# A two-layer decoder on one core: the experts' down products two slots later, one table of expert results, a token choice with fused sums, and norms that add their squares in halves

## The chip, the cores and the metric

The kernel runs as one program on one core of a Trainium2 chip. The metric is the device time of one launch in microseconds (us). In these texts PE is TensorE, DVE is VectorE, ACT is ScalarE, POOL is GpSimd and SP is SyncE, which issues most of the DMAs.

## The reference

Two post-norm decoder layers over 2048 tokens (8 sequences of 256) of width 512. Layer 0 is an attention whose keys and values are kept only for the most important tokens, a WKV recurrence, and a mixture of experts with 4-bit weights. Layer 1 is a causal attention, a cross attention and a dense feed-forward. A layer norm follows each part. What the change touches computes this:

```python
# sparse attention, layer 0: which tokens keep their key and value
importance = (x @ Wi + bi)[..., 0]
threshold = sorted_desc[:, tidx][:, None]          # tidx = int(256 * 0.2)
sparse_mask = (importance > threshold)
_, top_idx = jax.lax.top_k(importance, 32)         # and the 32 highest in any case
sparse_mask = jnp.maximum(sparse_mask, min_mask)

# layer norm, six times
m = jnp.mean(x, axis=-1); v = jnp.var(x, axis=-1)
y = (x - m) / jnp.sqrt(v + 1e-5)

# mixture: 16 experts, 4 per token, and a shared expert for all tokens
# each expert: silu(gate) * up, 512 -> 384, then down 384 -> 512, weights in fp4
```

## The kernel before

Activations lie transposed in SBUF: `g.xt` ("residual") holds features on the 128 partitions, in C = 4 blocks, and the 2048 tokens along the free axis. The program is a list of stages, each a Block with a barrier of all engines at its end. Within a stage the order of each engine is written out by hand, and counting semaphores tie the engines together.

**The token choice** (`sparse_select`). DVE has the importance of all tokens on every partition (`imp`), with the partition as the token asked about. It takes its own token's importance (`own`, 16 columns: 8 sequences times 2 halves) and fills whole tables `ge` (others at least as important) and `gt` (others more important), each 4096 numbers a partition, then reduces, subtracts, masks with `tri` (others that come earlier) and reduces again. The count of those ahead decides whether a token is kept and in which slot. PE waits for the result `sel`.

**The norms** (`layer_norm`, numbered 0 to 5 by `layer`). Four tiles of 512 tokens each. Per tile: PE averages over features by a product with a constant matrix (`mean`, 4 matmuls), DVE subtracts (`centre`), ACT squares, PE averages the squares (`var`, 4 matmuls), ACT takes Ln and then Exp for the inverse root, DVE multiplies (`scale`). The norms 2 and 3 have a `prepare_next`: POOL works on the next stage's weights beside them. Norm 4 has a `fill_vector`: DVE decodes weights of the feed-forward between its own steps.

**The routing** (`route`). It writes the tokens, as two fp16 parts that sum to the value times 64, to `rows_dram`, and the value times 64 in f32 (`scaled`) as `kept` to the second of two tables `sum_dram[0]` and `sum_dram[1]`. `g.rows` names, for each slot of a routed tile, the token's row. An empty slot names a row behind the 2048 tokens, the same for both halves of a tile.

**The experts** (`experts`). 55 tiles of 256 slots: 8 of the shared expert over all tokens, then 47 routed ones. The work of a tile j is cut into 6 steps o, and all engines walk the same slots s = 6 j + o. In a slot PE does `group` (8 matmuls for 128 hidden features, gate or up), then one `down` (3 matmuls of a tile before: one half of the slots, one third of the hidden features), and in slots 1 and 3 a `turn` (8 transposes of the next tile's rows). `item = NO * (j - 1) + o - 2` says which down. What leads to a down is a chain over engines: ACT and DVE scale and add the group's results (L1348, L1406), POOL adds the halves (L1261), ACT takes silu (L1354), DVE multiplies (L1414), ACT rounds (`high`, L1361), DVE takes the rest (`low`, L1419), which is what `h_ready` counts. `out` moves a finished tile from PSUM to `y`. For a shared tile SP stores it to `sum_dram[0]`; for a routed one POOL scatters its halves by indirect DMAs that add, half k into table k (L1252). POOL's `gather` (L1240) loads the rows of tile j + 3. SP loads the weights of tile j + 2 when tile j - 1 has finished its downs (ring of three).

**The combining** (`combine`). SP loads both tables, DVE adds them, PE turns the sums back and ACT divides by 64 into `g.xt`.

```python
for n in range(G_I * j, G_I * (j + 1)):                  # POOL, tile j
    if j < N:
        pool.wait_ge(ev_dve, 4 * (n + 1)); ...           # the add of L1261
    if n % G_I == 0 and N_SHARED <= j + 3 < N: gather(j + 3)
    if n % G_I == 1 and N_SHARED <= j - 2: scatter(j - 2)
```

## Time and profile before

| | |
|---|---|
| median of 3 runs | 2708.68 us (2708.18 to 2710.73) |
| profiled execution | 2711.14 us, its span 2709.3 us |
| busy share: PE, DVE, ACT, POOL | 75%, 67%, 49%, 35% |
| mean granted clock of PE | 0.893 of full speed |

A row of a timeline gives the start in us from the span's start, the busy time in us, the engine, the line and operation, what it writes from what it reads, how many like it are merged, and in brackets the idle time of the engine just before it and what ended it. Rows of "x8" are eight instructions in a row. A row of the windows gives the stretch and its length, then busy us with the number of instructions for PE, PE's weight loads, DVE, ACT and POOL, then the granted clock of PE, the mean busy share of the 16 DMA engines, and GB/s. A row of a DMA queue gives its packets, MB and the share of 16 engines' time that its packets took; q0 carries POOL's indirect DMAs, q1 those of SP.

### The profile page before, as it was taken

How to read it: one execution, taken by the hardware profiler on the slowest of the kernel's cores; microseconds unless marked ns; L12 is line 12 of the kernel's file. 1: busy time of each engine (PE TensorE's matmuls, PEld its weight loads, DVE VectorE, ACT ScalarE, POOL GpSimd, SP SyncE). 2: the span in 40 equal slices, each digit the busy share in tenths (PEclk: the TensorE clock that was granted, in tenths of full speed). 3: DMA queues.
4: the chain of work that ended last, by engine and by line, in shares of the span. 5: the costliest groups of instructions: out<-in, count | busy, mean ns of one | idle time of the engine just before them, and what ended most of it. 6: DMA issues, size and time to landing. Idle time of an engine off the chain costs nothing. (4 is left out here: it accounts for less than half of the span.)

```text
span 2709.3 us, 33393 instructions
## 1 busy us (share of the span) xinstructions
PE 2043.6 (75%) x12168; PEld 1270.0 (47%) x12203; DVE 1814.1 (67%) x2409; ACT 1326.7 (49%) x2139; POOL 953.4 (35%) x547
## 2 busy tenths in 40 slices
PE   2788765126498898988956899997994776789986
PEld 1456642012366666666633566663552332344442
DVE  4349883875776777777744356654443897999975
ACT  0013232655376776766734223323553885556656
POOL 1014443213245777777735122224111000443330
PEclk7888887668699999999987999998997998899998
DMA  3224655001637999999964000002334530000001
GB/s 141 62 93 159 241 189 221 0 0 44 235 102 246 254 251 262 247 261 256 251 152 169 0 1 1 1 1 109 92 80 140 187 118 1 0 1 1 1 0 62
DMA packets 123684, 313.63 MB, mean 116 GB/s; under 512 B 29569, under 2 KB 49537, under 8 KB 119810
## 3 DMA queue, kind: packets, MB, share of 16 engines
q1 hardware_dynamic: 102466, 260.69, 27.8%
q0 software_dynamic: 21056, 50.84, 9.5%
q8 instruction: 96, 1.57, 0.2%
q14 instruction: 66, 0.54, 0.1%
HBM read 219.59 MB, written 92.68 MB: 115 GB/s over the span
## 5 line engine op out<-in xcount | busy, mean ns | idle before, releaser
L1406 DVE SCALAR_TENSOR_TENSOR x_part<-x_group,x_scale,x_part 128x256 f32<-128x256 f32 x660 | 287.9, 477 | 144.2 <-ACT x_part L1348 137.5
L1295 PE MATMUL x_group<-x_xt,x_gu 128*128 128x256 f16 x2640 | 346.2, 275 | 2.1 <-ACT x_part L1348 1.2
L1348 ACT ACTIVATE x_part<-x_group,x_scale 128x256 f32<-128x256 f32 x660 | 276.1, 471 | 123.5 <-PE x_group L1295 117.5
L1261 POOL TENSOR_TENSOR x_part<-x_part 128x512 f32<-128x512 f32 x165 | 235.4, 1431 | 196.7 <-DVE x_part L1406 196.7
L1295 PEld LDWEIGHTS x_group<-x_xt,x_gu 128*128 128x128 fp8e4 x2640 | 237.0, 98 | 85.9 <-issue 32.4
L1312 PE MATMUL x_y_ps<-x_d_hi,x_h_hi 128*128 128x512 f32 x330 | 160.0, 485 | 68.8 <-DVE x_h_lo L1419 66.8
L2418 POOL TENSOR_TENSOR f_part<-f_part 128x1024 f32<-128x1024 f32 x44 | 120.4, 2737 | 188.0 <-DVE f_part L2445 188.0
L154 PE MATMUL mean_n<-residual,const_tables 128*128 128x512 f32 x160 | 79.3, 648 | 138.6 <-PEq L733 103.5
L1754 POOL TENSOR_TENSOR c_pt<-c_pt,const_tables 128x1024 f32<-128x1024 f32 x32 | 75.8, 2369 | 258.4 <-ACT c_pt L1728 258.4
L2316 PE MATMUL f_group<-f_x_hi,f_raw 128*128 128x512 f16 x352 | 138.9, 394 | 32.1 <-DVE f_part L2445 24.6
L1252 POOL DMA_INDIRECT mixed_rows<-x_y,moe_rows x94 | 150.1, 1597 | 31.0 <-issue 20.8
L2182 ACT ACTIVATE z_pt<-z_s 128x1024 f32<-128x1024 f32 x128 | 119.7, 1052 | 51.5 <-PE z_s L2153 50.4
L2445 DVE SCALAR_TENSOR_TENSOR f_part<-f_group,f_scale,f_part 128x512 f32<-128x512 f32 x176 | 123.9, 742 | 26.8 <-ACT f_part L2367 21.1
L2316 PE MATMUL f_group<-f_x_lo,f_raw 128*128 128x512 f16 x352 | 138.0, 392 | 0.0
L2367 ACT ACTIVATE f_part<-f_group,f_scale 128x512 f32<-128x512 f32 x176 | 111.0, 679 | 44.2 <-PE f_group L2316 44.0
L1312 PE MATMUL x_y_ps<-x_d_lo,x_h_hi 128*128 128x512 f32 x330 | 131.1, 397 | 0.0
L1312 PE MATMUL x_y_ps<-x_d_hi,x_h_lo 128*128 128x512 f32 x330 | 130.2, 395 | 0.0
L154 PEld LDWEIGHTS mean_n<-residual,const_tables 128*128 128x128 f32 x160 | 32.9, 209 | 181.6 <-issue 181.6
L1240 POOL DMA_INDIRECT x_row<-token_rows,moe_rows x94 | 102.5, 1091 | 21.5 <-issue 16.4
L1312 PEld LDWEIGHTS x_y_ps<-x_d_hi,x_h_hi 128*128 128x128 f32 x330 | 62.5, 189 | 98.0 <-DVE x_h_lo L1419 92.8
L199 ACT ACTIVATE squares_n<-centred_n 128x2048 f32<-128x2048 f32 x24 | 45.9, 1911 | 127.5 <-DVE centred_n L177 127.5
L2330 PE MATMUL f_y<-f_h_hi,f_w_hi 128*128 128x512 f32 x176 | 104.9, 596 | 3.2 <-DVE f_h_lo L2457 2.2
(331 smaller groups left out, 5042.3 us busy)
## 6 DMA issues: line engine op xcount, KB each, us to landing
x_d_hi<-down_hi SPq DMA_DIRECT2D x50, 768.0 KB, 5.7
x_d_lo<-down_lo SPq DMA_DIRECT2D x50, 768.0 KB, 5.9
x_gu<-codes_gu SPq DMA_DIRECT2D x50, 384.0 KB, 5.7
p_w<-d_s SPq DMA_DIRECT2D x17, 768.0 KB, 7.7
down_hi<-p_hi SPq DMA_DIRECT2D x17, 768.0 KB, 3.9
down_lo<-p_lo SPq DMA_DIRECT2D x17, 768.0 KB, 6.3
aux<-ct SPq DMA_DIRECT2D x2, 4096.0 KB, 16.3
cross_values<-y_v_out SPq DMA_DIRECT2D x16, 512.0 KB, 3.0
```

Source lines behind the costliest of these rows:

```text
L154: mm = pe.matmul(mean_ps[t % 2][:, :], g.const("mean"), tile(src, t)[:, c, :], start=c == 0, stop=c == C - 1)
L1252: pool.indirect_dma_start(out=g.sum_dram[k], out_offset=bass.IndirectOffsetOnAxis(ap=g.rows[:, at:at + 1], axis=0), in_=y[u][:, k, :], in_ ...
L1261: pool.tensor_tensor(x[:, 0, :, :], x[:, 0, :, :], x[:, 1, :, :], ALU.add).then_inc(summed, 1)
L1295: mm = pe.matmul(group_ps[s % 2][:, q, :], codes[:, q, col:col + P], xt[u][:, k, q, :], start=k == 0, stop=k == 1)
L1312: mm = pe.matmul(y_ps[half][:, :], x[u][:, k, rows], w[v][:, k, :], start=k == 0 and i == 0, stop=k == G_I - 1 and i == 2)
L1348: act.activation(part[n % PARTS][:, q, o % 2, :], group_ps[s % 2][:, q, :], ACT.Copy, scale=scale[v][:, o, q:q + 1]).then_inc(ev_act, 1)
L1406: dve.scalar_tensor_tensor(x, group_ps[s % 2][:, 2 + q, :], scale[v][:, o, 2 + q:3 + q], x, ALU.mult, ALU.add).then_inc(ev_dve, 1)
L2182: act.activation(pt[n % RING_P][:, :, :, :], s_ps[n % 3][:, :, :, :], ACT.Exp, scale=HDX ** -0.5)\
L2316: mm = pe.matmul(group_ps[c][:, :], codes[:, n, C * k + c, :], x[t % 2][:, c, :], start=i == 0, stop=i == 1)
L2367: act.activation(part[N % PARTS][:, c, k, :], group_ps[c][:, :], ACT.Copy, scale=scale[:, N % G_F, k, c:c + 1]).then_inc(ev_act, 1)
L2418: pool.tensor_tensor(x[:, 0, :, :], x[:, 0, :, :], x[:, 1, :, :], ALU.add).then_inc(summed, 1)
L2445: dve.scalar_tensor_tensor(x, group_ps[c][:, :], scale[:, N % G_F, k, c:c + 1], x, ALU.mult, ALU.add)\
```

## The change

It has four parts.

In `experts`, `DOWN_LAG = 4` takes the place of the 2 in the number of the down that a slot does. ACT's `out` moves from slot 0 to slot 2, DVE's from slot 2 to slot 4, and POOL's `scatter` from behind the second add of a tile to behind the third.

The two tables of results become one, with 128 spare rows for each half of a tile, so that the two halves' empty slots name different rows. The copy `kept` is dropped: `combine` loads the one table in 8 pieces, PE turns it, and DVE divides by 64 and adds to the residual in one instruction from PSUM. ACT has no part in it.

In the choice, each of the 16 columns has three SCALAR_TENSOR_TENSOR of 256 elements that compare, mask and sum in one instruction (`accum_out`), and the tables `ge` and `gt` are only written, in fp16. `later` (1 minus `tri`) is made ahead of it, while DVE waits for `imp`.

In the norms, DVE's `pair` adds the squares of blocks 0, 1 to those of 2, 3, in place, for the norms without `prepare_next` (0, 1, 4 and 5), and `var` is 2 matmuls there. PE does three tiles' `mean` before the first `var`, and DVE's order is written out anew. All six norms get an Ln of one column (`primed`) ahead of the wait for `var`.

```diff
@@ layer_norm
+        halved = prepare_next is None
+        base_pairs, ahead = g.pairs, 2 if halved else 1
...
             def var(t):
-                pe.wait_ge(squares_ready, base + t + 1)
+                if halved:
+                    pe.wait_ge(paired, base_pairs + t + 1)
+                else:
+                    pe.wait_ge(squares_ready, base + t + 1)
...
-                for c in range(C):
+                terms = C // 2 if halved else C
+                for c in range(terms):
...
-            mean(0)
+            for t in range(ahead):
+                mean(t)
             for t in range(NT):
-                if t + 1 < NT:
-                    mean(t + 1)
+                if t + ahead < NT:
+                    mean(t + ahead)
                 var(t)
...
+            def pair(t):
+                if halved:
+                    dve.wait_ge(squares_ready, base + t + 1)
+                    x = squares[t % 2]
+                    dve.tensor_tensor(x[:, 0:2, :], x[:, 0:2, :], x[:, 2:4, :], ALU.add).then_inc(paired, 1)
...
             for t in range(NT):
+                act.activation(primed[:, :], eps, ACT.Ln)
                 act.wait_ge(var_ready, base + t + 1)
@@ sparse_select
-                dve.tensor_tensor(ge[:, :, q, :], imp[:, :, :], mine, ALU.is_ge)
-                last = dve.tensor_tensor(gt[:, :, q, :], imp[:, :, :], mine, ALU.is_gt)
...
-            step(dve.tensor_reduce(n_gt, gt[:, :, :, :].rearrange("p b q j -> p (b q) j"), AX.X, ALU.add))
...
+            for n in range(2 * B):
+                b, q, mine = n // 2, n % 2, own[:, n:n + 1]
+                earlier = g.const("tri")[:, q * S:(q + 1) * S]
+                dve.scalar_tensor_tensor(ge[:, n, :], imp[:, b, :], mine, ones, ALU.is_ge, ALU.mult,
+                                         accum_out=n_ge[:, n:n + 1])
+                dve.scalar_tensor_tensor(gt[:, 0, n, :], imp[:, b, :], mine, earlier, ALU.is_ge, ALU.mult,
+                                         accum_out=ties[:, n:n + 1])
+                last = dve.scalar_tensor_tensor(gt[:, 1, n, :], imp[:, b, :], mine, later[:, q * S:(q + 1) * S],
+                                                ALU.is_gt, ALU.mult, accum_out=after[:, n:n + 1])
             step(last)
-            step(dve.tensor_tensor(ties, ties, n_gt, ALU.add))
+            step(dve.tensor_tensor(ties, ties, after, ALU.add))
@@ route
-                sp.dma_start(kept[:, n:n + 4, :], scaled[:, n:n + 4, :]).then_inc(stored, 16)
@@ experts
-                    pool.indirect_dma_start(out=g.sum_dram[k], out_offset=bass.IndirectOffsetOnAxis(ap=g.rows[:, at:at + 1], axis=0),
+                    pool.indirect_dma_start(out=g.sum_dram, out_offset=bass.IndirectOffsetOnAxis(ap=g.rows[:, at:at + 1], axis=0),
...
-                    if n % G_I == 1 and N_SHARED <= j - 2:
+                    if n % G_I == 2 and N_SHARED <= j - 2:
                         scatter(j - 2)
...
-                item = NO * (j - 1) + o - 2
+                item = NO * (j - 1) + o - DOWN_LAG
...
-                if o == 0 and 2 <= j < N + 2:
+                if o == DOWN_LAG - 2 and 2 <= j < N + 2:
                     out(j - 2)
...
-                if o == 2 and 2 <= j < N + 2:
+                if o == DOWN_LAG and 2 <= j < N + 2:
                     out(j - 2)
@@ combine
-    NTOK, GROUP = T // P, 4
+    NTOK, GROUP = T // P, 2
...
+                dve.scalar_tensor_tensor(x, turn_ps[n % 4][:, :, :], 1.0 / X_GAIN, x, ALU.mult, ALU.add).then_inc(out, 1)
```

PE in the expert stage, where tile 5 (its weights in `gu2`) is in its slots 2 and 3; `d_hi1` are the down weights of tile 4 and `d_hi0` those of tile 3. Before:

```order
L1312 MATMUL x_y_ps0<-x_d_hi1,x_h_hi0 128x512 [waits x_y0_out,x_h_ready,x_d_landed1]
L1312 MATMUL x_y_ps0<-x_d_hi1,x_h_lo0 128x512
L1312 MATMUL x_y_ps0<-x_d_lo1,x_h_hi0 128x512
L1295 MATMUL x_group1<-x_xt1,x_gu2 128x256 [waits x_ev_act]
L1295 MATMUL x_group1<-x_xt1,x_gu2 128x256 x3
L1295 MATMUL x_group1<-x_xt1,x_gu2 128x256 [waits x_ev_dve]
L1295 MATMUL x_group1<-x_xt1,x_gu2 128x256 x3
L1312 MATMUL x_y_ps0<-x_d_hi1,x_h_hi0 128x512 [waits x_h_ready]
```

and at the same place of the changed kernel:

```order
L1347 MATMUL x_y_ps1<-x_d_hi0,x_h_hi1 128x512
L1347 MATMUL x_y_ps1<-x_d_hi0,x_h_lo1 128x512
L1347 MATMUL x_y_ps1<-x_d_lo0,x_h_hi1 128x512
L1330 MATMUL x_group1<-x_xt1,x_gu2 128x256 [waits x_ev_act]
L1330 MATMUL x_group1<-x_xt1,x_gu2 128x256 x3
L1330 MATMUL x_group1<-x_xt1,x_gu2 128x256 [waits x_ev_dve]
L1330 MATMUL x_group1<-x_xt1,x_gu2 128x256 x3
L1347 MATMUL x_y_ps1<-x_d_hi0,x_h_hi1 128x512
```

The downs beside the same groups are those of two slots earlier: they end tile 3 where they began tile 4, and no wait for `h_ready` stands in these two slots.

POOL at the end of the expert stage, where the last tiles are scattered. Before:

```order
L1261 TENSOR_TENSOR x_part3<-x_part3 128x512 [waits x_ev_dve]
L1252 DMA mixed_rows0<-x_y0,moe_rows 2176x512 [waits x_y0_out,x_y_mixed1]
L1252 DMA mixed_rows1<-x_y0,moe_rows 2176x512 [waits x_y1_out]
L1261 TENSOR_TENSOR x_part0<-x_part0 128x512 [waits x_ev_dve]
L1252 DMA mixed_rows0<-x_y1,moe_rows 2176x512 [waits x_y0_out,x_y_mixed0]
L1252 DMA mixed_rows1<-x_y1,moe_rows 2176x512 [waits x_y1_out]
L1252 DMA mixed_rows0<-x_y0,moe_rows 2176x512 [waits x_y0_out,x_y_mixed1]
L1252 DMA mixed_rows1<-x_y0,moe_rows 2176x512 [waits x_y1_out]
```

and changed:

```order
L1296 TENSOR_TENSOR x_part3<-x_part3 128x512 [waits x_ev_dve]
L1296 TENSOR_TENSOR x_part0<-x_part0 128x512 [waits x_ev_dve]
L1287 DMA mixed_rows<-x_y0,moe_rows 2304x512 [waits x_y0_out,x_y_mixed1]
L1287 DMA mixed_rows<-x_y0,moe_rows 2304x512 [waits x_y1_out]
L1287 DMA mixed_rows<-x_y1,moe_rows 2304x512 [waits x_y0_out,x_y_mixed0]
L1287 DMA mixed_rows<-x_y1,moe_rows 2304x512 [waits x_y1_out]
L1287 DMA mixed_rows<-x_y0,moe_rows 2304x512 [waits x_y0_out,x_y_mixed1]
L1287 DMA mixed_rows<-x_y0,moe_rows 2304x512 [waits x_y1_out]
```

The scatter that stood between the second and third add of the last tile stands behind the third; all name one table.

DVE in norm 0. Before:

```order
L177 TENSOR_TENSOR centred0_n0<-residual,mean0_n0 128x2048 [waits ln_mean_ready]
L177 TENSOR_TENSOR centred1_n0<-residual,mean1_n0 128x2048 [waits ln_mean_ready]
L177 TENSOR_TENSOR centred2_n0<-residual,mean0_n0 128x2048 [waits ln_mean_ready]
L190 TENSOR_TENSOR residual<-centred0_n0,rs0_n0 128x4x512 [waits ln_rs_ready]
L177 TENSOR_TENSOR centred3_n0<-residual,mean1_n0 128x2048 [waits ln_mean_ready]
L190 TENSOR_TENSOR residual<-centred1_n0,rs1_n0 128x4x512 [waits ln_rs_ready]
L190 TENSOR_TENSOR residual<-centred2_n0,rs0_n0 128x4x512 [waits ln_rs_ready]
L190 TENSOR_TENSOR residual<-centred3_n0,rs1_n0 128x4x512 [waits ln_rs_ready]
```

and changed, where rows that write `squares` are the additions in halves:

```order
L186 TENSOR_TENSOR centred0_n0<-residual,mean0_n0 128x2048 [waits ln_mean_ready]
L186 TENSOR_TENSOR centred1_n0<-residual,mean1_n0 128x2048 [waits ln_mean_ready]
L193 TENSOR_TENSOR squares0_n0<-squares0_n0 128x1024 [waits ln_squares_ready]
L186 TENSOR_TENSOR centred2_n0<-residual,mean0_n0 128x2048 [waits ln_mean_ready]
L193 TENSOR_TENSOR squares1_n0<-squares1_n0 128x1024 [waits ln_squares_ready]
L186 TENSOR_TENSOR centred3_n0<-residual,mean1_n0 128x2048 [waits ln_mean_ready]
L193 TENSOR_TENSOR squares0_n0<-squares0_n0 128x1024 [waits ln_squares_ready]
L197 TENSOR_TENSOR residual<-centred0_n0,rs0_n0 128x4x512 [waits ln_rs_ready]
L193 TENSOR_TENSOR squares1_n0<-squares1_n0 128x1024 [waits ln_squares_ready]
L197 TENSOR_TENSOR residual<-centred1_n0,rs1_n0 128x4x512 [waits ln_rs_ready]
L197 TENSOR_TENSOR residual<-centred2_n0,rs0_n0 128x4x512 [waits ln_rs_ready]
L197 TENSOR_TENSOR residual<-centred3_n0,rs1_n0 128x4x512 [waits ln_rs_ready]
```

The first tile is scaled behind the fourth tile's subtraction, not ahead of it, and the second only when all four additions are done.

## Rows read from the trace of the kernel before

**Rows 1.** Windows: busy time by stretch, first a shared stretch, then one routed tile.

```profile
780.00:800.00 20.00, 17.93 (x141) 13.39 (x138) 13.82 (x34) 14.08 (x34) 10.41 (x9) 1.00 0.34 103
1200.00:1212.08 12.08, 10.87 (x82) 8.03 (x82) 9.25 (x23) 8.47 (x20) 9.31 (x7) 1.00 0.92 258
```

**Rows 2.** Timeline of PE in the expert stage: start us, us, engine line op.

```profile
738.07 0.50 PE L1312 MATMUL x_y_ps<-x_d_hi,x_h_hi 128*128 128x512 f32 x1 [1.76 <-DVE x_h_lo L1419]
...
833.29 0.50 PE L1312 MATMUL x_y_ps<-x_d_hi,x_h_hi 128*128 128x512 f32 x1 [1.48 <-DVE x_h_lo L1419]
...
1206.75 1.05 PE L1295 MATMUL x_group<-x_xt,x_gu 128*128 128x256 f16 x8
...
1208.33 0.62 PE L1279 MATMUL x_turn<-x_ident,x_row 128*128 128x128 f16 x8
1208.79 1.04 PE L1295 MATMUL x_group<-x_xt,x_gu 128*128 128x256 f16 x8
...
1212.62 0.50 PE L1312 MATMUL x_y_ps<-x_d_hi,x_h_hi 128*128 128x512 f32 x1 [1.21 <-DVE x_h_lo L1419]
...
1380.57 0.50 PE L1312 MATMUL x_y_ps<-x_d_hi,x_h_hi 128*128 128x512 f32 x1 [0.66 <-DVE x_h_lo L1419]
```

**Rows 3.** Timeline of POOL over one routed tile.

```profile
1209.43 1.28 POOL L1261 TENSOR_TENSOR x_part<-x_part 128x512 f32<-128x512 f32 x1 [1.49 <-DVE x_part L1406]
...
1213.77 1.27 POOL L1261 TENSOR_TENSOR x_part<-x_part 128x512 f32<-128x512 f32 x1 [0.36 <-DVE x_part L1406]
```

**Rows 4.** DMA queues over four routed tiles, 1200 to 1248.32 us.

```profile
q1 hardware_dynamic: 2892, 8.02, 48.1%
q0 software_dynamic: 1792, 4.33, 44.0%
```

**Rows 5.** Timeline of the expert stage's end, POOL and DVE.

```profile
1383.15 1.56 POOL L1252 DMA_INDIRECT mixed_rows<-x_y,moe_rows  x1
...
1384.19 0.88 DVE L1406 SCALAR_TENSOR_TENSOR x_part<-x_group,x_scale,x_part 128x256 f32<-128x256 f32 x2
...
1390.28 1.56 POOL L1252 DMA_INDIRECT mixed_rows<-x_y,moe_rows  x1 [2.41 <-DMA mixed_rows<-x_y,moe_rows]
```

**Rows 6.** Timeline of DVE in the token choice.

```profile
41.98 2.29 DVE L322 TENSOR_TENSOR s_ge<-s_imp,s_own 128x2048 f32<-128x2048 f32 x1
...
73.28 0.17 DVE L335 TENSOR_SCALAR s_small<-s_small 128x16 f32<-128x16 f32 x1
```

**Rows 7.** Timeline of DVE: two nearby kinds of instruction, 256 elements each.

```profile
687.56 0.69 DVE L1034 TENSOR_TENSOR_SCAN r_running<-const_tables,r_total 128x256 f32<-128x256 f32 x1
...
1200.74 0.87 DVE L1406 SCALAR_TENSOR_TENSOR x_part<-x_group,x_scale,x_part 128x256 f32<-128x256 f32 x2
```

**Rows 8.** Timeline of the combining stage, issue to last eviction.

```profile
1410.22 0.38 SPq L1485 DMA_DIRECT2D m_mixed<-mixed_rows  x1
...
1418.44 2.50 DVE L1492 TENSOR_TENSOR m_mixed<-m_mixed,m_kept 128x512 f32<-128x512 f32 x4 [24.42 <-DMA m_kept<-mixed_rows]
...
1424.75 3.64 PE L1501 MATMUL m_turn<-const_tables,m_mixed 128*128 128x128 f32 x16 [1.89 <-DVE m_mixed L1492]
...
1438.41 1.14 ACT L1508 ACTIVATE residual<-m_turn 128x512 f32<-128x512 f32 x2 [0.26 <-PE m_turn L1501]
```

**Rows 9.** Timeline of ACT and DVE in the first norm, and after it.

```profile
473.67 1.92 ACT L199 ACTIVATE squares_n<-centred_n 128x2048 f32<-128x2048 f32 x1 [2.17 <-DVE centred_n L177]
...
480.54 1.91 ACT L199 ACTIVATE squares_n<-centred_n 128x2048 f32<-128x2048 f32 x1 [1.01 <-DVE centred_n L177]
...
490.36 2.29 DVE L190 TENSOR_TENSOR residual<-centred_n,rs_n 128x2048 f32<-128x2048 f32 x1 [1.65 <-ACT rs_n L210]
...
493.19 0.20 ACT L784 ACTIVATE w_fade<-w_fade 128x4 f32<-128x4 f32 x1
```

**Rows 10.** Timeline of the third norm's end: DVE and POOL.

```profile
1470.10 7.24 DVE L190 TENSOR_TENSOR residual<-centred_n,rs_n 128x2048 f32<-128x2048 f32 x2 [1.48 <-ACT rs_n L210]
...
1482.07 4.49 POOL L1552 TENSOR_TENSOR c_wk<-c_wk,c_wkr 128x2048 f32<-128x2048 f32 x1
```

More of the change, by code:

```diff
@@ L178, in centre, with scale @@
                                   ALU.subtract).then_inc(centred_ready, 1)
-            if fill_vector is not None:
-                fill_vector(dve, 0)
-            centre(0)
-            centre(1)
-            for t in range(NT):
-                if t + 2 < NT:
-                    centre(t + 2)
-                if fill_vector is not None and t >= 1:
-                    fill_vector(dve, t)
+            def pair(t):
[3 more added lines that the diff above has]
+                    dve.tensor_tensor(x[:, 0:2, :], x[:, 0:2, :], x[:, 2:4, :], ALU.add).then_inc(paired, 1)
+            def scale(t):
                 dve.wait_ge(rs_ready, base + t + 1)
@@ L191, in _, with fill @@
                                   ALU.mult).then_inc(normed, 1)
+            def fill(t):
+                if fill_vector is not None:
+                    fill_vector(dve, t)
+            fill(0)
+            centre(0)
+            centre(1)
+            pair(0)
+            centre(2)
+            pair(1)
+            fill(1)
+            if halved:
+                centre(3)
+                pair(2)
+                scale(0)
+                pair(3)
+            else:
+                scale(0)
+                centre(3)
+            fill(2)
+            scale(1)
+            fill(3)
+            scale(2)
+            scale(3)
         @block.scalar
@@ L313, in _ @@
             dve.tensor_copy(wib[:, :, :], bc(wi[:, :], 2, [P, C, P])).then_inc(wib_ready, 1)
+            dve.tensor_scalar(later[:, :], g.const("tri"), -1.0, 1.0, ALU.mult, ALU.add)
             dve.wait_ge(imp_copied, NT)
@@ L922, in _ @@
             out = g.rows_dram[0:T, :].rearrange("(n p) f -> p n f", p=P)
[L923 to L926 removed]
+            for k in range(HALVES):
+                spare = slice(T + k * P, T + (k + 1) * P)
+                sp.dma_start(g.rows_dram[spare, :], a["one_row"][:, 0:ROW].to_broadcast([P, ROW])).then_inc(stored, 16)
+                sp.dma_start(g.sum_dram[spare, :], a["one_row"][:, 0:D].to_broadcast([P, D])).then_inc(stored, 16)
             for n in range(0, NTOK, 4):
@@ L1066, in _ @@
             dve.wait_ge(rows_found, 1)
-            step(dve.tensor_scalar(empty[:, :], row_ps, 0.0, g.const("spare"), ALU.is_equal, ALU.mult))
+            for k in range(HALVES):
+                last = dve.tensor_scalar(empty[:, k::HALVES], row_ps[:, k::HALVES], 0.0, g.const("spare")[:, k:k + 1],
+                                         ALU.is_equal, ALU.mult)
+            step(last)
             dve.scalar_tensor_tensor(g.rows[:, :], empty[:, :], -1.0, row_ps, ALU.add, ALU.add)
@@ L1480, in _ @@
         def _(sp):
+            rows = g.sum_dram[0:T, :].rearrange("(n p) f -> p n f", p=P)
             for i, s in enumerate(landed):
                 part = slice(i * GROUP, (i + 1) * GROUP)
-                for dst, src in ((mixed, g.sum_dram[0]), (kept, g.sum_dram[1])):
-                    rows = src[0:T, :].rearrange("(n p) f -> p n f", p=P)
-                    sp.dma_start(dst[:, part, :], rows[:, part, :]).then_inc(s, 16)
-        @block.vector
-        def _(dve):
-            for n in range(NTOK):
-                if n % GROUP == 0:
-                    dve.wait_ge(landed[n // GROUP], 32)
-                dve.tensor_tensor(mixed[:, n, :], mixed[:, n, :], kept[:, n, :], ALU.add).then_inc(summed, 1)
+                sp.dma_start(mixed[:, part, :], rows[:, part, :]).then_inc(s, 16)
         @block.tensor
@@ L1496, in _ @@
             for n in range(NTOK):
[L1497 removed]
+                if n % GROUP == 0:
+                    pe.wait_ge(landed[n // GROUP], 16)
                 if n >= 4:
```

57 lines of the change are left out of this document (23 added, 34 removed).

## The prediction

> **What bounds the kernel now.** I began with the page (busy shares, the slices, the groups), then took the waits of the expert stage, the timelines of the places that the diff touches, the windows for a price per tile, and the DMA queues. No engine is busy throughout: the page's 75% for PE is an average over stages that end on different things, so each edit is priced at its own place.
>
> The experts take a quarter of the time, 55 tiles in a row. In a routed tile of 12.08 us PE is busy 10.87, and DVE, ACT and POOL 9.3, 8.5 and 9.3; the DMA engines are at 0.92, against 0.34 in a shared stretch [rows 1]. What ends PE's idle time, once a tile, is DVE's `low`: the second down of a tile waits 1.21 us for it, behind a group [rows 2]. Without this wait a slot is a group and a down, 1206.75 to 1208.33, 1.58 us, and a turn 0.46 (to 1208.79): six slots and two turns make 10.4 us [rows 2]. So each tile loses about 1.7 us to a chain that passes ACT and DVE several times and POOL once, while every one of them has time left. The granted clock there is 1.00, the 2.4 GHz level [rows 1], so nothing is to be had from the clock.
>
> The other three places are serial. The choice is one chain on DVE from 41.98 to 73.28 us, with PE waiting [rows 6]. The combining starts its loads at 1410.22 and sees the first 2 MB land at 1418.44 [rows 8]. The norms are a chain over PE, DVE and ACT.
>
> **The experts, in four steps.** The three items of `down` that wait for `h_ready` come two slots later, and so do the two `out`s and the scatter: no distance between them changes, only that from `low` to its down, from one slot to three. Two slots are over 3.1 us, the wait 1.21, so it goes. What is late next? PE may run two slots ahead of the evictions of `group_ps`. By hand, with DVE's 9.25 us in a tile of 10.4, DVE has 1.1 us left [rows 1], and its heaviest slot (group, out, low, product) is followed by slots with less. ACT has more. So the floor of PE, 10.4 us, is reachable as far as compute goes.
> - Shared tiles: from the stall at 738.07 to that at 833.29 are 8 periods of 11.90 us [rows 2]. DMA is at 0.34, no limit. I take 10.55 a period: 8 x 1.35 = 10.8 us off.
> - Routed tiles: 833.29 to 1380.57 hold 45 periods, 12.16 on average [rows 2], 12.08 in steady state [rows 1]. Two limits stand close under that. POOL waits 1.49 and 0.36 us in a tile [rows 3], so its adds, gathers and scatters with their issue take 12.08 - 1.85 = 10.2 us. And the DMA engines: over four tiles (48.3 us) the packets took 48.1% and 44.0% [rows 4], that is 11.1 us a tile. The shares of the two queues sum to that of the windows, so packets of one do not lie beside packets of the other on an engine, and if their durations stay, 11.1 us is the least that a tile can take in the long run. It is not felt at once: weights are asked for some 13 slots before use, over 20 us, and a backlog of 11.1 - 10.5 a tile needs more than 20 tiles to use that up. I take 10.6 to 10.7 for the first half and 11.2 for the second, 10.95 on average: 45 x (12.08 - 10.95) = 50.9 us off.
> - The last group comes two downs earlier, 2 x 0.78 = 1.6 us off.
> - The end: the scatter that stood behind the second add of the last tile stands behind the third. Before, it was issued at 1383.15, and the next only at 1390.28, when its DMA had landed: three pairs, each some 7 us behind the other, end the stage [rows 5]. The last groups' eviction starts at 1384.19 and takes 0.88; with the add of 1.27 [rows 3] the chain of scatters starts near 1386.4, 3.3 us later. 3.3 us on.
>
> Sum of the experts: 10.8 + 50.9 + 1.6 - 3.3 = 60.0 us off. Bounds of the routed period: PE's 10.4 (75.6 us instead of 50.9) and 11.6, where the DMA share of 11.1 meets jitter (21.6).
>
> **The choice.** What goes is 31.3 us, 41.98 to 73.28 [rows 6]. What comes is 48 instructions of 256 elements and one addition of some 0.2. The trace has none that sums on the side. From below: a comparison of 2048 elements takes 2.29 us [rows 6], so 256 take at least 0.29, 13.7 us in all. From above: the scan, a DVE instruction that carries a value from element to element, takes 0.69 for 256 [rows 7], 33 us. The nearest in kind is the SCALAR_TENSOR_TENSOR of 256, two in 0.87 [rows 7], 0.44 with its own latency in it; behind each other they overlap, so I take 0.40: 19.2 + 0.2 = 19.4, and 11.9 us off (17.4 off to 2 on). The table `later` is made while DVE waits for `imp`, as it did before.
>
> Two statements of the Trainium skill speak against this part. "Vector Engine (DVE) Microarchitecture Reference", section "Points that are easy to get wrong", says that a SCALAR_TENSOR_TENSOR with two non-bf16 SBUF sources runs at half throughput, since no port is left for the accumulator's readback; and "VectorE: DVE Perf Modes", in its section on two Vector instructions with no wait between them, counts an operation that writes out its accumulator as two instructions. No run here shows either so far; by the first an instruction would take about twice its 0.29, an estimate of 0.58, and this part would give 3 us.
>
> **The combining.** Now 29.3 us (1410.22 to 1439.55) [rows 8]. Half the bytes, eight pieces of 512 KB instead of pairs of 1 MB. The first 2 MB land 8.2 us after the issue; a quarter of it lands after 8.2/4 = 2.1 at the least and I take 4.2. Then PE has 16 turns without a gap: four take 3.64 [rows 8], so 14.6, and the last eviction some 0.7: 19.5, 9.8 us off. PE is the bound of it, as the 4 MB land at twice the pace. The 16 additions of DVE that go, and ACT's copies, lay between; the new ones lie beside PE. The four stores of `kept` end long before the routing does, so dropping them gives nothing; one more small instruction on `empty` costs 0.1.
>
> **The norms.** In norm 0, ACT waits 2.17 and 1.01 us for DVE's subtraction, which waits for `mean`, which stood behind a `var` [rows 9]. With `mean` first and `var` half as long these 3.2 us go, and ACT, with three table loads and activations a tile, is the bound to the end. `primed` adds a small ACT instruction a tile; the nearest takes 0.20 [rows 9], 0.8 at most. So 3.2 - 0.8 leaves 2.4; I take 2.2 for the norms 0, 1 and 5, and 1.8 for norm 4, where DVE's decoding stands before its second scale: 8.4 off. The additions (DVE, four a norm, 1.2 each by half of a 2048-element product of 2.29 [rows 9]) lie beside ACT. Norm 2 ends with POOL, 1486.56 against DVE's 1477.34 [rows 10]: `primed` costs nothing. Norm 3 pays 0.6. Sum: 7.8 off.
>
> **The sum.** 60.0 + 11.9 + 9.8 + 7.8 = 89.5 us. Against the profiled execution's own 2711.1: 2621.6. The median of the runs is 2.4 below that one, so 2619.
>
> **The rivals.**
> 1. DMA is the bound of routed tiles throughout (11.2 to 11.6 a tile), through POOL: a scatter may not start before the last has landed, and POOL's adds wait behind it. For it: 0.92 at 12.08, and the second scatter already lands some 7 us after the first's issue [rows 1, 4, 5]. Against it: in a steady tile POOL waits for DVE alone [rows 3]. At 11.4: 30.6 instead of 50.9, 2639.
> 2. PE's floor is reached, the packets shorten or overlap: 10.45 a tile, 73 off, 2597. For it: q1's 8.02 MB in 48.1% of 48.3 us are 345 GB/s, q0's 4.33 in 44.0% only 204 [rows 4]; scatter packets may be mostly latency that a fuller queue hides.
> 3. The fused sums cost what the scan does, 0.69: 2 us on instead of 11.9 off, 2633.
> 4. The change doesn't do what it says: the wait for `low` comes back as a wait for evictions, because POOL's adds come behind two scatters in a row and silu and DVE follow. Period 11.8 or more: 12.6 instead of 50.9, 2657.
> 5. Slower. Scatters and weight loads meet in time, since weights are asked for two slots later as well; a pair of scatters then lands after more than a period, and POOL's wait sets the pace. The rest of the change gives 11.9 + 9.8 + 7.8 + 9.1 = 38.6, so it decides from 12.08 + 38.6/45 = 12.94 a tile on; with pairs of 13.3 us (now some 7) it would be 2725.
>
> **How the numbers follow.** Chances: the forecast (2606 to 2630) 0.42, DMA-bound 0.22, PE's floor 0.20, the scan's price 0.06, no gain in routed tiles 0.06, slower 0.03, and 0.01 for no change. The time is that of the forecast, 2619. The range takes in PE's floor and the dearer DMA case with the scan's price: 2592 to 2652. The forecast's own is 2606 to 2630. What a measurement of this kernel can tell from no change is about 0.2%, 5.4 us. Faster 0.96, same 0.01, slower 0.03.
>
> **What the changed profile would show.** In the routed stretch no wait of PE for `x_h_lo`, and a period near 10.9, with DMA over 0.97; if the period is 10.45, DMA under 0.97 refutes the fixed packet times; if it is 11.4, POOL's L1287 waits for its own DMA. Periods near 10.55 in shared tiles. 48 instructions in the choice, 19 us from first to last. The combining in 19.5 us with PE without gaps. 2.2 us less in norm 0, with no ACT wait for `centred`. The scatter chain at the end 3.3 us later behind the last group. Wrong it would be above all by the routed period: each 0.1 us is 4.5 us.

## The result, and the profile after

The changed kernel takes 2634.37 us (median of 3 runs, 2634.15 to 2637.72) against 2708.68; the ratio is 0.9728, 95% interval 0.9706 to 0.975. Forecast were 2619, in a range of 2592 to 2652; the measured time is 15 us above the forecast. The profiled execution took 2634.15 us with a span of 2632.2, that is 77.1 off the span where the sum had 89.5: 12.4 of the 15 us. Another 2.4 are what the forecast took off because the profiled execution of before stood that much above its median; after the change the two are level.

Where it came from, in us of the profiled spans. A term is read between two rows that both kernels have; copy k is DVE's one copy of `x_xt` for tile k. The forecast up to copy 13 is 8 shared periods and 4 routed ones (10.8 + 4.5), then 41 times 1.13.

| stretch | before | after | change | forecast |
|---|---|---|---|---|
| choice: first comparison to PE's `s_row` | 36.46 | 24.99 | -11.5 | -11.9 |
| norms 0, 1, 5: first subtraction to last scale | 30.47 | 27.43 | -3.04 each | -2.2 each |
| norm 4, the same | 30.47 | 27.91 | -2.6 | -1.8 |
| norm 3, the same | 30.47 | 30.65 | +0.2 | +0.6 |
| experts, copy 0 to copy 13 (shared, and the first routed) | 154.09 | 139.11 | -15.0 | -15.3 |
| experts, copy 13 to copy 54: 41 routed periods | 495.42 | 471.35 | -24.1 | -46.3 |
| last copy to the combining's first load | 39.26 | 43.91 | +4.7 | +1.7 |
| combining to norm 2's first `mean` | 29.64 | 16.19 | -13.5 | -9.8 |
| unchanged code elsewhere | | | -6.3 | 0 |

The row that fails is that of the routed tiles. Their period is 11.50 us, the same to 0.02 in nearly every tile, where it was 12.08 and the forecast had 10.95. The windows of after, a shared stretch and one routed tile (columns as in [rows 1]):

```profile
760.00:780.00 20.00, 20.00 (x160) 15.34 (x159) 15.27 (x38) 15.36 (x39) 10.57 (x10) 1.00 0.34 104
1157.27:1168.78 11.51, 10.87 (x86) 7.87 (x84) 10.02 (x23) 8.03 (x20) 9.06 (x7) 1.00 0.93 267
```

In the shared stretch PE has no gap left. In the routed tile the DMA share is 0.93 against 0.92, and POOL is busy for less than in [rows 1], but DVE has gone from 9.25 us to 10.02 in a shorter tile, with the same 23 instructions. PE's timeline of this tile has no wait for `x_h_lo` any more and two new ones. The first is put down to issue in PE's row, but the row of its weight load (PEld) names DVE's eviction:

```profile
1163.56 0.61 PE L1330 MATMUL x_group<-x_xt,x_gu 128*128 128x256 f16 x4 [0.33 <-issue]
1163.56 0.33 PEld L1330 LDWEIGHTS x_group<-x_xt,x_gu 128*128 128x128 fp8e4 x4 [0.61 <-DVE x_part L1441]
...
1167.32 0.61 PE L1330 MATMUL x_group<-x_xt,x_gu 128*128 128x256 f16 x4 [0.31 <-DVE x_part L1441]
```

DVE's timeline shows why the evictions are late, with POOL's beneath it:

```profile
1159.87 0.87 DVE L1441 SCALAR_TENSOR_TENSOR x_part<-x_group,x_scale,x_part 128x256 f32<-128x256 f32 x2 [1.35 <-ACT x_part L1383]
1160.66 1.72 DVE L1454 TENSOR_TENSOR x_h_lo<-x_h,x_h_hi 128x256 fp32r<-128x256 f32 x1
1162.30 0.41 DVE L1449 TENSOR_TENSOR x_h<-x_part 128x256 f32<-128x256 f32 x1
1162.64 0.86 DVE L1441 SCALAR_TENSOR_TENSOR x_part<-x_group,x_scale,x_part 128x256 f32<-128x256 f32 x2
...
1165.46 0.68 DVE L1454 TENSOR_TENSOR x_h_lo<-x_h,x_h_hi 128x256 fp32r<-128x256 f32 x1
...
1166.40 0.86 DVE L1441 SCALAR_TENSOR_TENSOR x_part<-x_group,x_scale,x_part 128x256 f32<-128x256 f32 x2
...
1168.48 0.42 DVE L1454 TENSOR_TENSOR x_h_lo<-x_h,x_h_hi 128x256 fp32r<-128x256 f32 x1
```

```profile
1157.27 1.63 POOL L1287 DMA_INDIRECT mixed_rows<-x_y,moe_rows  x1 [0.15 <-issue]
1159.21 1.58 POOL L1287 DMA_INDIRECT mixed_rows<-x_y,moe_rows  x1 [0.30 <-issue]
1160.25 1.84 POOL L1296 TENSOR_TENSOR x_part<-x_part 128x512 f32<-128x512 f32 x1
...
1164.57 1.28 POOL L1296 TENSOR_TENSOR x_part<-x_part 128x512 f32<-128x512 f32 x1
```

The same `low` takes 0.42, 0.68 and 1.72 us. The two long ones start while POOL's add runs and end 0.29 us after it does (the add ends at 1162.09 and `low` at 1162.38; 1165.85 and 1166.14). The evictions behind them end at 1163.50 and 1167.26, and PE's two waits end 0.06 us later. The kernel before had this once a tile, in DVE's and POOL's timelines; the add ends at 1207.93, `low` at 1208.23:

```profile
1207.26 0.97 DVE L1419 TENSOR_TENSOR x_h_lo<-x_h,x_h_hi 128x256 fp32r<-128x256 f32 x1
```

```profile
1206.08 1.85 POOL L1261 TENSOR_TENSOR x_part<-x_part 128x512 f32<-128x512 f32 x1
```

Over the stage `low` averaged 567 ns before (164 of them) and 840 ns after:

```profile
L1454 DVE TENSOR_TENSOR x_h_lo<-x_h,x_h_hi 128x256 fp32r<-128x256 f32 x164 | 137.7, 840 | 0.5 <-ACT x_h_hi L1396 0.5
```

From 1159.87 to 1170 DVE has hardly any idle time, and PE, two slots ahead of it, waits for its evictions.

The choice, in DVE's timeline (answers to [rows 6]); each sum has a row of its own:

```profile
40.67 0.48 DVE L359 SCALAR_TENSOR_TENSOR s_ge<-s_imp,s_own,const_tables 128x256 f16<-128x256 f32 x1
41.08 0.08 DVE L359 DVE_READ_ACCUMULATOR s_ge<-s_imp,s_own,const_tables 128x1 f32 x1
41.08 0.48 DVE L361 SCALAR_TENSOR_TENSOR s_gt<-s_imp,s_own,const_tables 128x256 f16<-128x256 f32 x1
...
60.29 0.18 DVE L366 TENSOR_TENSOR s_small<-s_small 128x16 f32<-128x16 f32 x1
```

48 instructions in 19.6 us, 0.41 from start to start. The combining (answers to [rows 8]):

```profile
1356.58 4.20 SPq L1516 DMA_DIRECT2D m_mixed<-mixed_rows  x8
1360.38 5.82 PE L1526 MATMUL m_turn<-const_tables,m_mixed 128*128 128x128 f32 x32 [25.23 <-DMA m_mixed<-mixed_rows]
...
1370.47 1.09 PE L1526 MATMUL m_turn<-const_tables,m_mixed 128*128 128x128 f32 x8 [0.20 <-DMA m_mixed<-mixed_rows]
...
1372.77 7.11 PE L158 MATMUL mean_n<-residual,const_tables 128*128 128x512 f32 x16 [1.21 <-PEq L1501]
```

Each of the last four pieces comes 1.3 to 1.4 us after the one before, and PE takes its two turns in 1.09 us and waits for the next. The first turns were slower: four of them took 3.8 us, 0.42 us a matmul against 0.27 later. The windows of PE's work on four turns before and of the first turns after show the same granted clock, 0.50 (the 1.2 GHz level); in the last turns it is 1.00 (2.4 GHz):

```profile
1424.75:1428.00 3.25, 3.25 (x15) 3.25 (x16) 1.75 (x3) 1.59 (x3) 0.00 (x0) 0.50 1.05 390
```

```profile
1360.38:1363.30 2.92, 2.86 (x12) 2.46 (x13) 1.39 (x2) 0.00 (x0) 0.00 (x0) 0.50 1.03 390
1369.17:1370.26 1.09, 1.08 (x8) 0.86 (x8) 1.08 (x3) 0.00 (x0) 0.00 (x0) 1.00 0.06 21
```

PE had been idle for 25.23 us ahead of the first turn, and for 1.89 us ahead of the four in [rows 8]. The norm, ACT and then DVE in norm 0 (answers to [rows 9]):

```profile
458.74 1.89 ACT L231 ACTIVATE squares_n<-centred_n 128x2048 f32<-128x2048 f32 x1
460.65 1.28 ACT L236 ACT_TABLE_LOAD   x1
461.95 0.20 ACT L236 ACTIVATE primed_n<-const_tables 128x1 f32<-128x1 f32 x1
462.06 0.67 ACT L241 ACTIVATE rs_n<-var_n,const_tables 128x512 f32<-128x512 f32 x1
```

```profile
447.14 2.29 DVE L186 TENSOR_TENSOR centred_n<-residual,mean_n 128x2048 f32<-128x2048 f32 x1 [24.30 <-PE mean_n L158]
...
474.56 2.29 DVE L197 TENSOR_TENSOR residual<-centred_n,rs_n 128x2048 f32<-128x2048 f32 x1 [1.74 <-ACT rs_n L243]
```

Behind its second squaring ACT has no wait any more in this norm; `primed` lies 0.11 us before the next start. The tail of the experts, POOL's timeline (answers to [rows 5]):

```profile
1328.87 1.56 POOL L1287 DMA_INDIRECT mixed_rows<-x_y,moe_rows  x1 [0.15 <-issue]
...
1336.18 1.55 POOL L1287 DMA_INDIRECT mixed_rows<-x_y,moe_rows  x1 [3.89 <-DMA mixed_rows<-x_y,moe_rows]
...
1343.48 1.55 POOL L1287 DMA_INDIRECT mixed_rows<-x_y,moe_rows  x1 [3.88 <-DMA mixed_rows<-x_y,moe_rows]
```

### The profile page after: what moved, and what is told of

Its sections match the earlier page's. It is cut to its first block and busy times, and to the rows that moved or that the text cites. A ratio compares the mean times of both kernels' runs of the same rounds, so it can differ in the third digit from the quotient of the medians.

```text
span 2632.2 us, 33369 instructions
## 1 busy us (share of the span) xinstructions
PE 2009.7 (76%) x12104; PEld 1245.7 (47%) x12139; DVE 1850.9 (70%) x2514; ACT 1297.3 (49%) x2147; POOL 945.4 (36%) x547
## 5 line engine op out<-in xcount | busy, mean ns | idle before, releaser
L1330 PE MATMUL x_group<-x_xt,x_gu 128*128 128x256 f16 x2640 | 362.0, 275 | 33.4 <-DVE x_part L1441 17.9
L1330 PEld LDWEIGHTS x_group<-x_xt,x_gu 128*128 128x128 fp8e4 x2640 | 229.4, 98 | 140.6 <-issue 60.0
L1383 ACT ACTIVATE x_part<-x_group,x_scale 128x256 f32<-128x256 f32 x660 | 264.5, 472 | 10.8 <-PE x_group L1330 10.6
L1396 ACT ACTIVATE x_h_hi<-x_h 128x256 fp32r<-128x256 f32 x165 | 68.8, 417 | 166.6 <-DVE x_h L1449 141.0
L1454 DVE TENSOR_TENSOR x_h_lo<-x_h,x_h_hi 128x256 fp32r<-128x256 f32 x165 | 138.2, 837 | 0.5 <-ACT x_h_hi L1396 0.5
## 6 DMA issues: line engine op xcount, KB each, us to landing
aux<-ct SPq DMA_DIRECT2D x2, 4096.0 KB, 15.3
```

The lines of the kernel that those rows point to most:

```text
L1330: mm = pe.matmul(group_ps[s % 2][:, q, :], codes[:, q, col:col + P], xt[u][:, k, q, :], start=k == 0, stop=k == 1)
L1383: act.activation(part[n % PARTS][:, q, o % 2, :], group_ps[s % 2][:, q, :], ACT.Copy, scale=scale[v][:, o, q:q + 1]).then_inc(ev_act, 1)
L1454: dve.tensor_tensor(h_lo[j % 2][:, n % G_I, :], h[n % 2][:, :], h_hi[j % 2][:, n % G_I, :].bitcast(F32), ALU.subtract).then_inc(h_ready, 1)
```

## The experiments

All times are medians, beside runs of the kernel before on the same chip (2709.9 to 2710.3). "Split" is the changed kernel with the edit of `split_scatter`.

| run | us | routed period, mean of 41 | DVE's `low`, mean ns from 700 to 1330 us |
|---|---|---|---|
| changed kernel | 2634.4 | 11.50 | 840 |
| lag2 | 2672.1 | 12.07 | 553 |
| lag3 | 2635.0 | 11.50 | 822 |
| low_one_input | 2620.8 | 11.17 | 406 |
| low_product_one | 2596.6 | 10.63 | 409 |
| split_scatter | 2595.9 | 10.52 | 445 |
| lag2_split | 2661.8 | 11.86 | 415 |
| split_early_weights | 2586.3 | 10.55 | 467 |
| split_light_weights | 2587.7 | 10.44 | 433 |
| best | 2586.4 | | |

**lag2: the lag undone.**

```diff
-    DOWN_LAG = 4
+    DOWN_LAG = 2
...
-                    if n % G_I == 2 and N_SHARED <= j - 2:
+                    if n % G_I == 1 and N_SHARED <= j - 2:
```

> The changed kernel with one part undone: the downs one slot behind again (DOWN_LAG 2), both outs two slots earlier and the scatter behind the second add of a tile. Theory (the later down gave 39 us between the first and the last tile and took 4 to 5 us back at the tail): routed tiles at 12.08 us again instead of 11.50, shared tiles at 11.8 instead of 10.4 to 10.6, so about 35 us longer than the changed kernel, 2669. Rival (part of the gain in the stage comes from the single table or its spare rows, not from the lag): routed tiles stay clearly under 12.0 and the time under 2660.

2672.1 us, 37.7 longer, routed 12.07 and shared 11.8. The stage's gain is the lag's; the one table and its spare rows have no part in it.

**lag3: one slot more, not two.** `DOWN_LAG = 3`, scatter as in lag2.

> The changed kernel with the down one slot later than before instead of two (DOWN_LAG 3), outs in slots 1 and 3, and the scatter behind the second add of a tile, as before the change. Theory: two slots, 3.1 us, still cover the 1.2 us that the down waited for low; the adds, gathers and scatters of POOL stand as before, where low was held up by 0.56 us a tile instead of 1.6, so DVE is busy 9.2 to 9.5 us and the routed period is 10.7 to 11.1, the tail 4 us shorter: about 2608. Rival (DMA-bound): 11.5, 2630. Rival (a lag of one slot more is not enough): PE waits for x_h_lo again, 11.5 to 12.

2635.0 us, 11.50 a tile and `low` at 822 ns. The tail is 4.5 us shorter, as expected, and given back ahead of copy 13 (2.2 us) and of the stage (2.5). So the scatter's new place is not what holds `low` longer: once PE stops waiting, DVE and POOL fall into the same pattern with the scatters behind the second add too. That part of the theory fell.

**low_one_input: `low` with one operand from SBUF.**

```diff
-                dve.tensor_tensor(h_lo[j % 2][:, n % G_I, :], h[n % 2][:, :], h_hi[j % 2][:, n % G_I, :].bitcast(F32),
-                                  ALU.subtract).then_inc(h_ready, 1)
+                    dve.tensor_reduce(h_lo[j % 2][:, n % G_I, :], h[n % 2][:, :].rearrange("p (m o) -> p m o", o=1),
+                                      AX.X, ALU.add).then_inc(h_ready, 1)
```

> The changed kernel, but DVE's low is a reduction over one element of h alone: same length, one SBUF input instead of two. It leaves the subtraction of h_hi out. Theory (low is held up until POOL's add beside it has ended, 1.3 and 0.3 us in a tile, DVE then runs behind and PE waits for its evictions): low takes about 0.41 us everywhere, DVE is busy 8.4 instead of 10.0 us in a tile, and the routed period falls from 11.50 to 10.4 to 10.9; with 10.6 some 40 us less, about 2594. Rival (the DMA engines, busy 0.93 of the time, set the 11.50): low is short, but the period stays at 11.5 and the time at 2634. Rival (POOL's own chain of adds, gathers and scatters sets it): the same 11.5, with POOL waiting for nothing.

2620.8 us, period 11.17. The time fell by 13.6 us, a third of the 40 that were expected. DVE's timeline, and the add of POOL beside it:

```profile
1152.38 0.41 DVE L1455 TENSOR_REDUCE x_h_lo<-x_h 128x256 fp32r<-128x256 f32 x1
1152.70 1.40 DVE L1449 TENSOR_TENSOR x_h<-x_part 128x256 f32<-128x256 f32 x1
```

```profile
1151.98 1.83 POOL L1296 TENSOR_TENSOR x_part<-x_part 128x512 f32<-128x512 f32 x1
```

`low` now runs beside the add at its full pace. The hold went to the product behind it, the next instruction with two operands from SBUF: 1.40 us, again to 0.29 after the add's end.

**low_product_one: the product as well.** Its `tensor_tensor` becomes the same kind of reduction.

> The changed kernel with both DVE instructions that read two operands from SBUF in the chain made into reductions over one element with one operand: low (leaves out the subtraction of h_hi) and product (leaves out the multiplication by up). Lengths stay 0.41 us when undisturbed. Theory (any DVE instruction with two SBUF inputs that meets POOL's add is held until the add ends; with low alone changed, the product took over 0.98 and 0.27 us of the hold, and the period only fell to 11.17): no hold is left, DVE is busy 8.4 to 8.6 us a tile, period 10.4 to 10.6, about 2593 us. Rival (POOL's pair of scatters makes the add late, and the late sum itself, through silu and product, sets the period whatever DVE does): low and product are both 0.41 but the period stays at 11.0 or more, 2612 or above.

2596.6 us, period 10.63 (29 of the 41 lie under 10.6, many at 10.3), both instructions at 0.41. DVE and POOL at the same place of a tile:

```profile
1076.74 0.41 DVE L1456 TENSOR_REDUCE x_h_lo<-x_h 128x256 fp32r<-128x256 f32 x1
1077.07 0.41 DVE L1449 TENSOR_REDUCE x_h<-x_part 128x256 f32<-128x256 f32 x1
```

```profile
1075.12 1.58 POOL L1287 DMA_INDIRECT mixed_rows<-x_y,moe_rows  x1 [0.30 <-issue]
1076.17 1.86 POOL L1296 TENSOR_TENSOR x_part<-x_part 128x512 f32<-128x512 f32 x1
```

POOL's order is that of the changed kernel, its add still stands behind two scatters and has the same 1.8 us, and still the tile is 0.87 us shorter. So neither POOL's chain nor the DMA engines made the 11.50: the hold on DVE did.

**split_scatter: the same by the order alone, with nothing left out.**

```diff
-                    if n % G_I == 2 and N_SHARED <= j - 2:
-                        scatter(j - 2)
+                    if n % G_I in (1, 2) and N_SHARED <= j - 2:
+                        scatter(j - 2, n % G_I - 1)
```

The second argument is the half.

> The changed kernel, but POOL scatters the first half of a tile behind the second add and the second half behind the third add, so that no add stands behind two scatters. Theory (POOL's add of the next tile comes late behind the pair of scatters, and so falls on DVE's low): the add is on time, low is held up less, routed period 10.7 to 11.1, about 2612 us. Rival (DMA-bound): 11.5 and 2634. Rival (the halves then wait for the landing of the tile before, as the last scatter is issued later against the next first one): POOL waits for its own DMA in every tile, period 12 or more, above 2650.

2595.9 us, 38.5 less than the changed kernel and more than was expected. Each add now stands behind one scatter or the gathers, POOL's timeline:

```profile
1152.13 1.28 POOL L1297 TENSOR_TENSOR x_part<-x_part 128x512 f32<-128x512 f32 x1 [0.56 <-DVE x_part L1442]
1153.57 1.57 POOL L1288 DMA_INDIRECT mixed_rows<-x_y,moe_rows  x1 [0.16 <-issue]
1154.91 1.54 POOL L1297 TENSOR_TENSOR x_part<-x_part 128x512 f32<-128x512 f32 x1
```

and the adds end as DVE comes to `low`, or before: the first `low` starts at 1153.27, 0.14 us ahead of the add's end, and takes 0.43 us, the second starts at 1156.96, 0.5 us behind it, and takes 0.41. What is left of PE's waits from 900 to 1250 us is that for `x_scale`, 3.8 us in 6 times.

**lag2_split: the split without the lag.** `DOWN_LAG = 2` in the split version.

> The version with split scatters, with the down back at its old place (DOWN_LAG 2, outs in slots 0 and 2); the halves of a tile are scattered behind the second and the third add. Theory (two separate limits: the wait of PE for low, which only the lag removes, and the hold of DVE beside POOL, which only the split removes): PE waits for x_h_lo again, about 1.2 us a tile, routed period 11.7 to 12.0, about 2660 to 2672 us. Rival (the scatters in a pair were what made low late before the change as well, so the split alone would have done): period 10.5 to 11, under 2625 us.

2661.8 us. `low` is short, and PE waits for it as before, once a tile, in its timeline:

```profile
1115.39 0.50 PE L1348 MATMUL x_y_ps<-x_d_hi,x_h_hi 128*128 128x512 f32 x1 [1.01 <-DVE x_h_lo L1455]
```

Without the lag the split gives 10.3 us, with it 38.5. The lag gives 37.7 alone and 65.9 with the split. Two limits stood one behind the other, and the change removed the first.

**split_early_weights and split_light_weights: what the DMA engines have to do with it.**

```diff
                 if N_SHARED <= j + 2 < N:
-                    e = expert(j + 2)
-                    gate_up(j + 2, e)
-                    down(j + 2, e)
+                    gate_up(j + 2, expert(j + 2))
+                if N_SHARED <= j + 1 < N:
+                    down(j + 1, expert(j + 1))
```

> The version with split scatters, and SP asks for the gate and up weights of tile j + 2 ahead of the down weights of tile j + 1, so they are not queued behind the wait for y_done, which the lag moved two slots back. In the split version PE waits for x_scale in some tiles (3.8 us from 900 to 1250 us) and periods of 10.42 alternate with 10.98. Theory (the scale is only late, as it is asked for 9 slots ahead): the waits go, period 10.42 throughout, 4 us less than 2596. Rival (the DMA engines, busy 0.99 of the time, are the limit and the wait only moves to another transfer): within 1 us of 2596.

The other loads one third of `d_lo` for routed tiles, the rest of the split version unchanged.

> The version with split scatters, with the low part of the down weights of routed tiles loaded for one third only (256 KB instead of 768 KB a tile, two thirds of the values are those of an earlier expert). Theory of the prediction (packet times are a load on the DMA engines that ends up as the limit near 11.1 us a tile): refuted already by 10.52; what is left of it is the wait for x_scale, which goes with a quarter of the weight bytes, period 10.42, about 2592 us, DMA share 0.8. Rival (no DMA limit at all, the waits come from the order of issue): the same 2596 with the same waits.

2586.3 and 2587.7 us. The windows from 900 to 1250 us, of early and then of light:

```profile
900.00:1250.00 350.00, 349.62 (x2719) 263.38 (x2717) 288.97 (x731) 269.76 (x662) 302.33 (x232) 1.00 1.00 293
```

```profile
900.00:1250.00 350.00, 350.00 (x2752) 266.58 (x2750) 285.86 (x736) 273.32 (x671) 303.99 (x235) 1.00 0.91 244
```

With a sixth of the bytes gone the period is 10.44 and nearly without jitter; with all of them it is 10.52 or 10.55, whatever the order of asking. So near 10.5 us the DMA engines do share the limit, for 0.1 us a tile: 3.3 of the light version's 8.2 us lie in the 41 periods, 3.8 ahead of them. The waits for `x_scale` went with the earlier asking, as expected, but waits of POOL for its own DMA grew instead (16.2 us in 20 times, 8.3 in 12 in the split version), so the steady part gained nothing. Of the early version's 9.6 us, 8.4 come from elsewhere: copy 8 to copy 13 takes 61.1 us in the split version, where POOL's first scatter waits 7.26 us for the last shared tile's store, issued by SP behind weights, and 52.7 in the early one, where it waits for no DMA.

**looks and mean_order: the small terms.** The first leaves `primed` out, adds eight SCALAR_TENSOR_TENSOR without a sum, and loads the combining in four pieces; the second has `ahead = 1` for all norms. Each ran once; `looks` took 2639.0 us, with eight instructions more in the choice.

> Three small edits of the changed kernel in stages that don't touch each other, each read from its own stage. (1) The six Ln of one column (primed) are gone. Theory: in a norm bound by ACT each costs its 0.11 us of pitch and hides nothing, since the table load stood ahead of the wait before the change too, so norm 0 is 0.4 us shorter; rival: it takes the table load off the path, and without it the norm is 1 us or more longer. (2) Eight SCALAR_TENSOR_TENSOR of 256 elements without a sum stand among the 48 with one. Theory: start to start both take 0.41 us, so the sum costs nothing; rival: the plain one takes 0.33 or less and the accumulator is paid for. (3) The combining loads four pieces of 1 MB instead of eight of 512 KB. Theory: the stage is bound by its 4 MB at some 400 GB/s, so it ends about one piece's worth of turns later, 1 to 2.5 us; rival: bound by PE's turns, the first piece lands 2 us later and all else follows by as much or more.

Norm 0 is 27.06 us instead of 27.42, and so are norms 1 and 5; norm 3 is 30.47 instead of 30.65. There `primed` costs 0.36 and 0.18 us and hides nothing. In norm 4 it is the other way: 28.14 us without it, 27.91 with it. Without it ACT starts its last load of the Ln table only when DVE, busy with its decoding, has scaled a tile. With `primed` that load lies ahead of the wait. ACT in norm 4 of `looks`:

```profile
2220.98 1.28 ACT L240 ACT_TABLE_LOAD   x1 [1.10 <-DVE residual L197]
```

The plain instruction and the one with a sum, in DVE's timeline:

```profile
41.30 0.49 DVE L360 SCALAR_TENSOR_TENSOR s_plain<-s_imp,s_own,const_tables 128x256 f16<-128x256 f32 x1
41.70 0.48 DVE L361 SCALAR_TENSOR_TENSOR s_ge<-s_imp,s_own,const_tables 128x256 f16<-128x256 f32 x1
42.10 0.09 DVE L361 DVE_READ_ACCUMULATOR s_ge<-s_imp,s_own,const_tables 128x1 f32 x1
42.10 0.48 DVE L363 SCALAR_TENSOR_TENSOR s_gt<-s_imp,s_own,const_tables 128x256 f16<-128x256 f32 x1
```

0.40 us from start to start for either. With four pieces the combining takes 18.3 us instead of 16.2, as expected.

> The changed kernel with PE's order in the norms as before (one mean ahead of a var, not two), and the squares still added in halves. Theory: the mean ahead is what lets DVE subtract in time; a var of half the length stands ahead of it now, so ACT waits for centred about 1.8 us less than before the change did, 3.2 - 1.8 = 1.4 us or less in norm 0, which is then 28 to 29 us from the first subtraction to the last scale (27.42 with both, 30.47 before). Rival: the halved var alone removes all of the wait, 27.4.

Norm 0 is 39.45 us, neither 28 nor 27.4, and the kernel 2680.6 in its one run, 46 us longer than the changed one. DVE's subtraction, in its timeline:

```profile
451.47 1.22 DVE L193 TENSOR_TENSOR squares_n<-squares_n 128x1024 f32<-128x1024 f32 x1
461.15 2.29 DVE L186 TENSOR_TENSOR centred_n<-residual,mean_n 128x2048 f32<-128x2048 f32 x1 [8.47 <-PE mean_n L158]
463.36 1.22 DVE L193 TENSOR_TENSOR squares_n<-squares_n 128x1024 f32<-128x1024 f32 x1
```

The third `mean` stands behind a `var` that waits for `pair`, and DVE's second `pair` stands behind the subtraction that waits for that `mean`: PE and DVE take turns instead of overlapping. The halves and the second `mean` ahead are one change and can't be told apart as two gains.

**best: the early version without `primed`.**

> The version with split scatters and early gate and up weights, without the six Ln of one column in the norms. Theory: 24 times 0.11 us, of which norm 2 (bound by POOL) returns nothing, so 2 us less than 2586.3, about 2584; rival: no difference that can be measured.

2586.4 us (2583.3 to 2587.7), no difference to the early version's 2586.3. Its norms 0, 1 and 5 are 0.35 us shorter each and norm 3 0.17, but norm 4 is 0.25 longer; the 1.0 us that this leaves is less than its runs differ by. The ratio to before is 0.9539 (0.9526 to 0.9552), 48 us under the changed kernel.

## Why the prediction came out as it did

The time fell in the stated range, 4 us above the forecast's own 2606 to 2630, but not by the mechanism that the sum held. An experts' term 25.6 us too large was half made up for by 13.2 us that others gave more than their terms, 6.3 of it in code that the change doesn't touch. This balance was luck.

- **Shared tiles**: right. Eight periods, from the second copy to the tenth, went from 93.3 to 82.1 us, 11.3 off where 10.8 stood.
- **Routed tiles**: the step that failed is "So the floor of PE, 10.4 us, is reachable as far as compute goes", with DVE's 9.25 us taken from [rows 1] as a fixed amount. It is no fixed amount: `low` and the product are as long as POOL's add leaves them. Before, PE's wait set the rhythm, and one `low` a tile was held for 0.56 us; with that wait gone the hold is 1.31 + 0.26. Removing it (low_product_one, 10.63), or its cause in the order (split_scatter, 10.52), comes within 0.1 to 0.2 us of the floor of 10.4. The term measured 24.1 us of 46.3 for 41 periods.
- **The DMA bound of 11.1**: wrong as a bound. Packet times shrank with the tile: 93% of 11.5 us is 10.7, and in split_scatter 99% of 10.52 is 10.4. Rival 2 had this right (packets shorten or overlap). Rival 1 names nearly the period that came, 11.4, with the wrong cause; POOL's scatters waited for no DMA in steady tiles, only twice at the end.
- **Rival 4** is nearest in kind: adds behind two scatters, and evictions late. Split_scatter shows that the pair matters, and lag3 (11.50 with the pair one add earlier) that its new place does not. But low_product_one reaches 10.63 with the adds just as late, so it isn't silu and DVE following a late add. The link was the hold, which neither the sum nor a rival had.
- **The tail**: +4.7 instead of +1.7. The chain of scatters itself kept its length (27.1 us from its first issue to the first load, now 27.7). Its start came 4.0 us later against the last copy, 3.3 forecast; the 1.6 us for the two earlier downs don't exist, since the chain hangs on POOL's last add and not on PE's last down.
- **The choice**: right, 0.41 for 0.40. The rival of 0.69 is out. Of the Trainium skill's two statements, that of "Vector Engine (DVE) Microarchitecture Reference", section "Points that are easy to get wrong", on half throughput does not hold here: 0.40 us with a sum and without, where the estimate by it was 0.58. That of "VectorE: DVE Perf Modes", on an accumulator output as two instructions, agrees with the rows: there is a second row, of 0.08 us, and it adds no time.
- **The combining**: mechanism wrong, size 13.5 for 9.8. The 3.64 us for four turns in [rows 8] were PE's pace at a granted clock of 0.50, and the sum took it for all 16 turns. After the change only the first four, 3.8 us, run at it; at 1.00 PE does two turns in 1.09 and waits for data. The bound is the 4 MB, at 385 to 401 GB/s from 1360 to 1368 us.
- **The norms**: mechanism right, size 3.04 for 2.2. `primed` was charged 0.8 a norm; it costs 0.36 in norms 0, 1 and 5, and in norm 4 it gives 0.24 back. The rows show two table loads and three activations a tile.
- **Routing**: within the 6.3 us of unchanged code, and not read apart. In those 6.3 are 1.3 us ahead of the choice and 1.5 in the first product behind norm 2 (10.08, then 8.62). That product, never edited, took 8.6 to 10.2 us in the thirteen profiles, with a granted clock of 0.71 before and 0.83 after. Ahead of the choice it is the 32 matmuls of the importance, 16.70 us and then 15.45 (15.4 to 17.0 in the thirteen). So these two change from one execution to another and are no gain of the change; the other 3.5 us stay open.

## What to carry to other kernels

An engine's busy time is no constant of its work where two engines share a path: before trusting the slack of DVE, look for instructions of the same shape with several durations, and at what POOL does beside the long ones. When a wait is removed, the pattern of such meetings is dealt anew, and where each helper DMA stands between POOL's adds can be worth as much as the wait itself (38 us each here). A pace of PE that was read at one granted clock is no price for work that may run at the other.
